# Attention in units of two key tiles: wide exponentials over two score banks, and PE's steps in pairs

## What is computed

```python
q = x @ Wq                      # x: layer norm of the input, 2 x 64 queries
k, v = jnp.split(context @ Wkv, 2, axis=-1)       # 16 heads of 64
k = concatenate((null_key, k)); v = concatenate((null_value, v))
q = jnp.tanh(q)
k = jnp.tanh(k)
sim = jnp.einsum('bhid,bhjd->bhij', q, k) * scale
attn = jax.nn.softmax(sim, axis=-1)
out = jnp.einsum('bhij,bhjd->bhid', attn, v)      # then out @ Wout + bout, added to x
```

## Time and profile before

| | us |
|---|---|
| median of 3 runs | 217.09 |
| lowest and highest of them | 215.47, 217.73 |
| the profiled execution | 214.31 |
| its span, first to last instruction | 212.5 |
| PE busy in it | 195.8 |
| DVE busy | 146.0 |
| ACT busy | 120.6 |
| POOL busy | 39.1 |

### The profile page before, as it was taken

How to read it: one execution, slowest core, us unless ns; L and a number is a source line. 1 busy time by engine, 2 the same in 40 slices (tenths; PEclk the granted TensorE clock), 3 DMA queues, 4 the chain that set the end, 5 groups by cost and what they waited for, 6 DMA issues and landing times.

```text
span 212.5 us, 4137 instructions
## 1 busy us (share of the span) xinstructions
PE 195.8 (92%) x1627; PEld 146.2 (69%) x1629; DVE 146.0 (69%) x249; ACT 120.6 (57%) x221; POOL 39.1 (18%) x40
## 2 busy tenths in 40 slices
PE   6895679999999999999999999999988899999991
PEld 1793578898988889888988877956755334635560
DVE  3459798889788799998988869833873737124313
ACT  3197678788888888878888864004631123331300
POOL 4139202204022040220311700020401400000001
PEclk9999999999999999999999999999999999999999
DMA  5896669971102011010000695999999400000000
GB/s 170 286 390 173 144 191 349 369 199 51 52 2 97 3 49 52 0 52 0 2 3 0 232 386 176 324 382 377 378 377 377 160 0 0 3 0 0 3 0 28
DMA packets 22853, 31.02 MB, mean 146 GB/s; under 512 B 1953, under 2 KB 18866, under 8 KB 22834
## 3 DMA queue, kind: packets, MB, share of 16 engines
q1 hardware_dynamic: 22834, 30.76, 43.2%
HBM read 29.57 MB, written 0.13 MB: 140 GB/s over the span
## 4 chain that ended last, share of the span: by engine, by line
PE 53%; issue 21%; DVE 13%; ACT 4%; DMA 3%; POOL 2%; SPq 1%; POOLq 0%; DVEq 0%
PE ps L1008 34%; PE ps L1042 6%; DVE keys L734 5%; DMA w_k_stage<-in_Wkv 3%; PE ps L1082 2%; PE ps L1096 2%; DVE ex_l L700 2%; PE ps L1188 1%; DVE mixT L744 1%; PE ps L996 1%; DVE q_split L725 1%; PE ps L1069 1%; PE ps L1172 1%; PE ps L1227 1%; DVE ex_sum L755 1%
## 5 line engine op out<-in xcount | busy, mean ns | idle before, releaser
L734 DVE SCALAR_TENSOR_TENSOR keys<-ps,keys 64x512 f16<-64x512 f32 x64 | 44.1, 689 | 7.1 <-ACT keys L573 5.7
L1008 PE MATMUL ps<-ctxT_h,w_k_h 128*128 128x256 f32 x128 | 39.4, 308 | 2.5 <-DVE keys L734 2.1
L573 ACT ACTIVATE keys<-ps 64x512 f16<-64x512 f32 x64 | 37.8, 591 | 1.8
L1008 PE MATMUL ps<-ctxT_h,w_k_l 128*128 128x256 f32 x128 | 36.6, 286 | 0.0
L1008 PE MATMUL ps<-ctxT_l,w_k_h 128*128 128x256 f32 x128 | 36.6, 286 | 0.0
L1008 PEld LDWEIGHTS ps<-ctxT_h,w_k_h 128*128 128x128 f32 x128 | 24.8, 194 | 4.2 <-issue 3.0
L569 ACT ACTIVATE ps<-ps 128x512 f32<-128x512 f32 x32 | 18.6, 582 | 14.7 <-PE ps L1008 14.7
L700 DVE TENSOR_TENSOR ex_l<-ps,ex_h 128x512 fp32r<-128x512 f32 x32 | 22.1, 691 | 6.7 <-ACT ps L603 6.1
L1008 PE MATMUL ps<-ex_h,ctx_h 128*128 128x512 f32 x64 | 25.7, 401 | 0.0
L1008 PE MATMUL ps<-ex_l,ctx_h 128*128 128x512 f32 x64 | 25.3, 395 | 0.0
L1008 PEld LDWEIGHTS ps<-ctxT_l,w_k_h 128*128 128x128 f32 x128 | 25.0, 195 | 0.0
(11 more groups left out here) (175 smaller groups left out, 260.2 us busy)
## 6 DMA issues: line engine op xcount, KB each, us to landing
w<-in_fc1T SPq DMA_DIRECT2D x8, 1024.0 KB, 12.3
w<-in_fc SPq DMA_DIRECT2D x8, 1024.0 KB, 11.9
stage_t<-in_ctxT SPq DMA_DIRECT2D x8, 256.0 KB, 5.0
stage_n<-in_ctx SPq DMA_DIRECT2D x8, 256.0 KB, 4.6
w_k_stage<-in_Wkv SPq DMA_DIRECT2D x4, 256.0 KB, 6.2
mixT<-in_Wq SPq DMA_DIRECT2D x2, 512.0 KB, 6.2
q_two<-q_split SPq DMA_DIRECT2D x8, 128.0 KB, 4.0
w_v<-in_Wkv SPq DMA_DIRECT2D x1, 1024.0 KB, 5.4
```

The source lines that it names most:

```text
L573: nc.scalar.activation(keys[rows, u % 2, PK * i:PK * (i + 1), r], full[rows].rearrange("p (j n) -> p j n", j=PK), ACT.Copy, scale=UNIT).th ...
L734: V.scalar_tensor_tensor(out=keys[other, u % 2, PK * i:PK * (i + 1), r], in0=ps[mine, K_BANK + kp % 2].rearrange("p (j n) -> p j n", j=PK) ...
L1008: last = MM(dst, lhs[i], rhs[j], start=start and m == 0, stop=stop and m == len(parts) - 1)
```

## The change

PE, ACT and DVE go through the loop in units of two steps. Steps 0 and 1 stay single. From unit 1 on, ACT waits for the scores of both steps and takes one exponential of 1024 columns over banks 6 and 7 into two slots of `ex_h`, and one in place; then come the two `keys_tanh`. DVE takes one rest of 1024 columns, then two sums, then two `low_keys`. From unit 2 on PE issues two `scores`, two `project_keys`, and the two `weighted_sum` of the unit before. Each of the wide operations adds 2 to its semaphore when it is done. Besides, SP issues the loads of `ctxT` one block earlier against those of `ctx`, and the first of them ahead of the loads of `b2`; DVE casts `ctxT` between the unit's two `low_keys`, and POOL takes the rest of `ctxT` ahead of that of `ctx`.

```diff
--- before.py
+++ after.py
@@ -431,14 +431,17 @@
 
             spread_queries(0)
             spread_queries(1)
+            load_ctxT(2)
+            load_ctx(2)
             for e in range(E):
                 half = SLOTS * (e % 2)
                 sp.dma_start(b2[half:half + SLOTS, e // 2, :],
                              a["b2"][e:e + 1, :].broadcast_to([SLOTS, D])).then_inc(ld_small, 16)
+            load_ctxT(3)
             sp.dma_start(w_v[:], a["Wkv"][:, INNER:2 * INNER].rearrange("(c p) n -> p c n", p=P)).then_inc(ld_wv, 16)
             sp.dma_start(w_out[:], chunked("Wout")).then_inc(ld_wv, 16)
-            load_ctxT(2)
-            load_ctx(2)
+            load_ctx(3)
+            load_ctxT(4)
             sp.dma_start(w_lq[:], chunked("lWq")).then_inc(ld_lin, 16)
             sp.dma_start(w_lk[:], chunked("lWk")).then_inc(ld_lin, 16)
             sp.dma_start(w_lv[:], chunked("lWv")).then_inc(ld_lin, 16)
@@ -447,9 +450,10 @@
             sp.dma_start(w_gk1[:], chunked("Wgk1")).then_inc(ld_lin, 16)
             sp.dma_start(w_gk2[0:LR + 1], a["Wgk2b"]).then_inc(ld_lin, 16)
             sp.dma_start(w_route[:], chunked("wg")).then_inc(ld_lin, 16)
-            for n in range(3, B * NC):
-                load_ctxT(n)
+            for n in range(4, B * NC):
                 load_ctx(n)
+                if n + 1 < B * NC:
+                    load_ctxT(n + 1)
             for e in range(E):
 
 
@@ -512,9 +516,9 @@
                     pool.wait_ge(null_sums, 2)
                     low_ctx(0)
                     for n in range(1, B * NC):
-                        low_ctx(n)
                         if n + 1 < B * NC:
                             low_ctxT(n + 1)
+                        low_ctx(n)
                     pool.wait_ge(ld_null_v, 16)
                     nc.gpsimd.tensor_scalar(null_ex[:], null_ex[:], null_v[:], None, ALU.mult).then_inc(null_values, 1)
                     pool.wait_ge(ld_const, 16)
@@ -593,7 +597,7 @@
                                      ACT.Exp, scale=DH ** -0.5).then_inc(null_ready, 1)
             keys_tanh(2)
 
-            for s in range(STEPS):
+            def exponentials(s):
                 act.wait_ge(s_psum, s + 1)
                 r = s % NE
                 if s >= NE:
@@ -601,8 +605,23 @@
                 full = ps[:, S_BANK + s % 2]
                 nc.scalar.activation(ex_h[:, r], full, ACT.Exp, scale=SCORE_SCALE)
                 nc.scalar.activation(full, full, ACT.Exp, scale=SCORE_SCALE).then_inc(e_ready, 1)
-                if s + AHEAD < STEPS:
-                    keys_tanh(s + AHEAD)
+
+            def both_exponentials(u):
+                act.wait_ge(s_psum, KT * (u + 1))
+                if u >= NE // KT:
+                    act.wait_ge(mix_done, KT * (u + 1) - NE)
+                r = KT * u % NE
+                full = ps[:, S_BANK:S_BANK + KT]
+                nc.scalar.activation(ex_h[:, r:r + KT], full, ACT.Exp, scale=SCORE_SCALE)
+                nc.scalar.activation(full, full, ACT.Exp, scale=SCORE_SCALE).then_inc(e_ready, KT)
+
+            for s in range(KT):
+                exponentials(s)
+                keys_tanh(s + AHEAD)
+            for u in range(1, NU):
+                both_exponentials(u)
+                for kp in range(KT * u + AHEAD, min(KT * (u + 1) + AHEAD, STEPS)):
+                    keys_tanh(kp)
             act.preload_act_table_set("natural_log_exp_and_others")
             for g in range(G):
 
@@ -771,30 +790,40 @@
             low_keys(1)
             high_ctx(0)
 
-            for s in range(STEPS):
-                u, t = divmod(s, KT)
-                b, c, g = units[u]
+            def low_exponentials(s):
                 r = s % NE
                 dve.wait_ge(e_ready, s + 1)
                 if s >= NE:
                     dve.wait_ge(mix_done, s - NE + 1)
                 low_part(ex_l[:, r], ps[:, S_BANK + s % 2], ex_h[:, r]).then_inc(el_ready, 1)
-                if s == 1:
-                    add_to_sum(0)
-                if s >= 1:
+
+            def both_low(u):
+                r = KT * u % NE
+                dve.wait_ge(e_ready, KT * (u + 1))
+                if u >= NE // KT:
+                    dve.wait_ge(mix_done, KT * (u + 1) - NE)
+                low_part(ex_l[:, r:r + KT], ps[:, S_BANK:S_BANK + KT], ex_h[:, r:r + KT]).then_inc(el_ready, KT)
+
+            low_exponentials(0)
+            low_keys(2)
+            low_keys(3)
+            low_exponentials(1)
+            add_to_sum(0)
+            add_to_sum(1)
+            low_keys(4)
+            for u in range(1, NU):
+                b, c, g = units[u]
+                n = b * NC + c
+                both_low(u)
+                for s in range(KT * u, KT * (u + 1)):
                     add_to_sum(s)
-
-                if s == 0:
-                    low_keys(2)
-                if s + AHEAD < STEPS:
-                    low_keys(s + AHEAD)
-
-                n = b * NC + c
-                if t == 0 and g == G - 1 and n + 1 < B * NC:
+                for kp in range(KT * u + AHEAD, min(KT * (u + 1) + AHEAD, STEPS)):
+                    low_keys(kp)
+                    if g == G - 1 and n + 2 < B * NC and kp == KT * u + AHEAD:
+                        high_ctxT(n + 2)
+                if g == G - 1 and n + 1 < B * NC:
                     high_ctx(n + 1)
-                if t == KT - 1 and g == G - 1 and n + 2 < B * NC:
-                    high_ctxT(n + 2)
-                if t == 0 and u >= 2 and units[u - 2][1] == NC - 1:
+                if u >= 2 and units[u - 2][1] == NC - 1:
                     evacuate(u - 2)
 
             dve.wait_ge(ld_small, 16 * (5 + E))
@@ -1121,19 +1150,27 @@
                 MM(ps[:, NULL_BANK[j]], null_kt[:], qT[:, 4 * j:4 * j + 4].rearrange("p j t -> p (j t)"), start=True,
                    stop=True).then_inc(null_psum, 1)
             project_keys(2)
-            LAG = 2
-            for s in range(STEPS):
-                if s == LAG:
-                    pe.wait_ge(null_ready, 2)
+            for s in range(KT):
                 scores(s)
-                if s + AHEAD < STEPS:
-                    project_keys(s + AHEAD)
-                if s == STEPS - 1:
+                project_keys(s + AHEAD)
+            scores(2)
+            pe.wait_ge(null_ready, 2)
+            weighted_sum(0)
+            scores(3)
+            project_keys(5)
+            project_keys(6)
+            weighted_sum(1)
+            for u in range(2, NU):
+                for s in range(KT * u, KT * (u + 1)):
+                    scores(s)
+                for kp in range(KT * u + AHEAD, min(KT * (u + 1) + AHEAD, STEPS)):
+                    project_keys(kp)
+                if u == NU - 1:
 
                     pe.wait_ge(k_ready, 2 * STEPS)
                     denominators(0)
-                if s >= LAG:
-                    weighted_sum(s - LAG)
+                for s in range(KT * (u - 1), KT * u):
+                    weighted_sum(s)
             weighted_sum(STEPS - 2)
             pe.wait_ge(e_ready, STEPS)
             denominators(1)
```

## The result

| | before | after |
|---|---|---|
| median of the timed runs, us | 216.28 (4 runs) | 224.25 (4 runs) |
| lowest and highest | 215.34, 217.73 | 223.19, 225.35 |
| profiled execution, its span | 214.31, 212.5 | 223.19, 221.4 |

The ratio is 1.0363, with a 95% interval of 1.0272 to 1.0454: the changed kernel is slower, by 8.0 us of the medians and 8.9 us of the profiled executions. The forecast was 225.5 us in a range of 222.5 to 229.0.

A forecast was written before the change was run, and what follows sets the result against it. TensorE's own work bounds the old kernel at 6.76 us per two steps; the change builds a 7.15 us chain. Entry +1.8, thirteen units at 7.15, batch change 0.5 and exit give +8.4 on 217.09: 225.5 us, range 222.5 to 229.0.

The forecast's parts named there:

- the ring: Closed path from a unit's first scores through ACT and DVE to the next scores: 7.15 us against 6.76 of PE work.
- first scores to exponential: First links of a unit: first scores 0.47 us, then second scores to the start of the exponential 0.67.
- first to second exponential: ACT link: 0.50 us for 512 columns plus 0.43 for another 512, together 0.93.
- to the rest: Link from the second wide exponential on ACT to the start of DVE's wide rest: 1.05 us.
- Entry: Loop start, where paired order begins: scores(4) start at 37.27 us instead of 35.48, +1.8.
- Change of batch: Two casts and an evacuation meet in one DVE unit, 2.24 us against 1.7 idle: 0.5 over, once.
- Exit: From scores(30) to the end of DVE's last sum 5.66 us; after slack, output matmuls move by +8.4.
- The wide instructions: 1024-column exponentials and rest over two score banks, costed by slopes of narrower rows: 0.43 and 0.53 us more.
- What the change gives back: PE's waits for `ctxT_l`, 0.42 us and its like, between scores(4) and scores(30), go.
- PE as the bound: Rival: the path falls under 6.76 us and PE runs on, no change that can be told, about 218.4; chance 0.07.
- a wide one costs as much as two narrow ones: Rival: wide operations save nothing, making the chain 7.37 us, +11.7, about 228.8; chance 0.10.
- The rule: Grouping helps saturated engines, splitting helps unsaturated ones causing gaps; the prediction said the trace sides with the second half.

The follow-up runs named there:

- run 2: Changed kernel with one-step exponentials on ACT again, each waiting for its own scores; rests stay wide: median 219.21 us, ratio 1.0137 to the kernel before.
- run 4: Changed kernel with one-step rests on DVE and the exponentials still wide: 7.22 us a unit, profiled execution 225.34 us.
- run 3: Changed kernel with one-step exponentials and one-step rests, paired order and moved loads kept: median 215.13 us, ratio 0.9962 to the kernel before.
- run 7: Kernel before with only the changed order of loads on SP, casts on DVE and rests on POOL: median 214.26 us, ratio 0.9878.
- run 8: Run 3 with batch 0's second evacuation on ACT and 8 useless matmuls on PE before the first scores: median 213.71 us, ratio 0.9861 to before.
- run 1: Changed kernel with the low keys of a unit's first key step ahead of the two sums on DVE: median 221.09 us, ratio 1.0222 to before.
- run 5: Changed kernel with an unread 128x512 DVE sum added between the two sums and the low keys: 7.80 us a unit, profiled 231.81 us.
- run 6: Changed kernel with the same unread DVE sum added behind the second key step's low keys: 7.21 us a unit, profiled 224.38 us.

## Why the prediction was right

**What bounds the kernel, and the ring.** Right, link by link. Predicted against measured, us: first scores to exponential 1.14 and 1.14; first to second exponential 0.93 and 0.92; to the rest 1.05 and 1.11; rest to sum 1.14 and 1.14; two sums 1.43 and 1.43; keys 1.41 and 1.41; to the next scores 0.05 and 0.06. The one link that is off is ACT to DVE: 0.09 us pass between the recorded end of the wide exponential and the start of the wide rest, where the narrow pair showed 0.03. That is 13 x 0.06 = 0.8 us of the sum. It goes with the width of the rest and not of the exponential: a wide rest starts 0.09 us behind a narrow exponential too (run 2), and a narrow rest 0.03 behind a wide one (run 4). Also, DVE idles 1.79 us only in the units without casts and 0.87 in the others, which are half of them, where I had said 1.7 in most.

**The terms.** Entry: scores(2) to scores(4) took 8.70 where the sum had 8.54. Change of batch: 7.57 - 7.21 = 0.36 where it had 0.5. Exit: 5.71 where it had 5.66, and the slack of 0.2 us behind it was used up, PE waiting for the first normalised product where it had not. The output matmuls start at 145.13, 9.1 us later than before, where the forecast had 8.4; the tail is the same, 76.3 against 76.5.

**The wide instructions.** 1027 and 1020 ns for the exponentials, 1.22 to 1.23 us for the rest: the slopes of narrower rows hold over two score banks. The saving against two narrow ones is real, 0.92 us from start to start where two narrow exponentials take 1.0, and 1.14 where two narrow rests take 1.21 (run 4). It is smaller than what waiting for the second scores costs: the narrow exponentials of run 2 take longer together and are done 0.3 us earlier.

**What the change gives back.** Right in kind, too small by the timed runs. I had counted PE's waits for `ctxT_l` at under 1 us; the moves alone brought 0.8 us in the trace and 1.9 us in the medians. So the change is the sum of two parts of unequal sign: the loop in units of two steps costs 224.25 - 214.26 = 10.0 us (by the two ratios to before, 1.0363 and 0.9878, 10.5), some 9 of it for the wide operations and some 0.9 for the paired order (runs 3 and 7), and the moved loads give 1.9 back. The traces agree: run 7 against the changed kernel, from scores(2) to scores(4) 6.75 against 8.70, over the stretch 86.45 against 94.14, from scores(30) to the output matmuls 13.28 against 13.85, together 10.2.

**Where the number owes something to luck.** The ring was 0.8 us too short in the sum and the gain of the moved loads 1.1 us too small; these misses have opposite signs, which is why +8.4 came so near to the measured +8.0. And of the 1.25 us between the forecast of 225.5 and the median of 224.25, 0.8 is the base: I had started from 217.09, the median of the kernel before became 216.28.

**The rivals.** PE as the bound came to pass only where both wide operations were split. That a wide one costs as much as two narrow ones did not: the numbers stand above.

**The rule.** The Trainium skill's page Perfetto Trace Analysis, section Optimizing Scalar/DVE Operations, has it that where ScalarE and VectorE are not saturated but cause gaps on others, breaking up their instructions may get the work done sooner. Runs 2 and 3 are that rule carried out, and gave 0.3 and 0.6 us a unit. Run 4 is it too, and gave nothing: the rests alone, broken up, had nothing to overlap with.

## What to carry to other kernels

Before operations are joined on an engine with idle time, write down the ring through all engines from one unit's start to the next one's, and compare its length with the work of the bounding engine: here 6.3 us in narrow steps and 7.21 in wide ones, against 6.65. Joining pays in busy time of an engine and costs in the time until its first result is out. An operation's place in the ring decides what it costs: 0.69 us of DVE work cost 0.58 a unit in it and nothing behind it, but for the one unit in which DVE had no idle time. And one change may hold several: the moved loads were worth keeping. The paired order was not shown to be: by itself it cost 0.9 us, and with its overload at the change of batch mended (run 8) it cannot be told from the old order.

## What the runs showed of the hardware

**The clock at the start of the loop.** PE stands idle in front of the first scores, since the keys come late (in run 2 the load of the queries is last). What followed differed from execution to execution. The windows from 20 to 26 us of run 7 and run 8 (stretch; length; busy us of PE, its weight loads, DVE, ACT, POOL; granted clock; DMA share; GB/s):

```profile
20.00:22.00 2.00, 0.22 (x2) 0.02 (x1) 1.94 (x3) 1.69 (x3) 1.89 (x2) 1.00 0.02 7
22.00:24.00 2.00, 1.45 (x22) 1.45 (x23) 0.92 (x2) 0.85 (x3) 0.90 (x1) 0.85 0.85 187
24.00:26.00 2.00, 2.00 (x19) 1.91 (x18) 1.59 (x3) 0.65 (x2) 0.39 (x1) 0.50 0.74 208
```

```profile
20.00:22.00 2.00, 1.91 (x10) 0.70 (x8) 1.94 (x3) 1.74 (x3) 1.84 (x2) 1.00 0.07 23
22.00:24.00 2.00, 1.51 (x24) 1.51 (x25) 0.86 (x2) 0.85 (x3) 0.96 (x1) 1.00 0.86 192
24.00:26.00 2.00, 1.13 (x22) 0.96 (x20) 1.65 (x3) 1.52 (x4) 0.33 (x1) 1.00 0.42 89
```

In run 7 the clock fell to half, 1.2 GHz, behind an idle time of 2.33 us. It did in runs 1, 2 and 4 as well, behind 2.3 to 2.6 us. In these four scores(2) start at 29.96 to 30.20 us, in the six other profiled executions at 28.44 to 29.32. The kernel before and run 3 stood idle for the same 2.33 us and kept 2.4 GHz, and so did the changed kernel and runs 5 and 6 behind 1.6 us. So the idle time alone does not say what the clock does. With PE busy there, and idle for 0.58 us only, run 8 kept it, in the one execution that has a trace. In the timed runs, which have a mean clock and no trace, it was under full speed in four of six, so the filling either does not hold always or the clock falls elsewhere too. This stays open.

**Instructions over two banks.** A ScalarE or VectorE instruction of 1024 columns that reads two score banks took what its columns say: 1.02 and 1.22 us, against 0.60 and 0.69 for 512.

**The start behind another engine.** A rest of 1024 columns started 0.09 us after the recorded end of the exponential that released it, whether that had 1024 columns (changed kernel) or 512 (run 2), and one of 512 columns 0.03 to 0.04 us after it (runs 3 and 4). The cause was not looked for.
